# Mean embedding and projection: the running sum of rows in SBUF, low halves in one operation, seven product banks

## What is computed

```python
valid = sequence_ids < emb_table.shape[0]
safe_ids = jnp.where(valid, sequence_ids, 0)
seq_emb = emb_table[safe_ids] * valid[..., None]
denom = jnp.maximum(valid.sum(axis=1, keepdims=True), 1.0)
user_repr = seq_emb.sum(axis=1) / denom
logits = user_repr @ proj_w + proj_b
```

## Time and profile before

| | us |
|---|---|
| median of 3 runs | 642.86 (642.55 to 642.87) |
| the profiled execution | 643.35 |
| its span, first to last instruction | 641.6 |
| PE busy, 2602 matmul records | 609.1 (95%) |
| DVE busy | 407.9 (64%) |
| POOL busy | 233.6 (36%) |
| ACT busy | 137.6 (21%) |

### The profile page before, as it was taken

One profiled execution on the slowest core, in us unless ns is written; L12 is line 12 of the kernel. 1 busy time (PEld: TensorE's weight loads), 2 busy tenths in 40 slices (PEclk: granted clock), 3 DMA queues, 4 the chain that ended last, 5 costly groups with the idle time before them and its releaser, 6 DMA issues.

```text
span 641.6 us, 7583 instructions
## 1 busy us (share of the span) xinstructions
PE 609.1 (95%) x2602; PEld 476.1 (74%) x2602; DVE 407.9 (64%) x723; ACT 137.6 (21%) x153; POOL 233.6 (36%) x227
## 2 busy tenths in 40 slices
PE   1878799989999999999999999999999999999997
PEld 0326558777778787788788788888888888888886
DVE  7977958989878898697786454333333333344442
ACT  7605426132122131300200221110011111211210
POOL 5777777777764767566550000000000000000000
PEclk9999989999999999999999999999999999999999
DMA  9979999999998999798793398454555555566632
GB/s 311 388 259 331 380 390 293 373 329 318 315 296 298 305 291 313 236 323 249 236 341 121 97 288 260 127 173 161 177 176 177 176 177 176 171 185 201 223 127 103
DMA packets 77703, 158.31 MB, mean 247 GB/s; under 512 B 9287, under 2 KB 65042, under 8 KB 77658
## 3 DMA queue, kind: packets, MB, share of 16 engines
q1 hardware_dynamic: 60378, 110.30, 50.7%
q0 software_dynamic: 17280, 47.47, 23.2%
HBM read 115.70 MB, written 51.20 MB: 260 GB/s over the span
## 4 chain that ended last, share of the span: by engine, by line
PE 75%; DVE 13%; DMA 6%; issue 5%; ACT 1%; DVEq 1%; POOL 0%; POOLq 0%; ACTq 0%
PE acc L801 70%; DVE sums L539 5%; DMA rows<-in_L_rec_emb_table_dram,index 4%; PE turned L757 2%; DMA w_raw<-in_L_rec_proj_w_dram 2%; DVE w_lo L597 2%; DVE key L496 1%; DVE w_lo L595 1%; DVE top L492 1%; PE acc L806 1%; ACT w_hi L416 1%; DVE stage L609 1%; PE turned L749 1%; DVE mean L584 0%; PE turned L732 0%
## 5 line engine op out<-in xcount | busy, mean ns | idle before, releaser
L347 POOL DMA_INDIRECT rows<-in_L_rec_emb_table_dram,index x208 | 224.1, 1077 | 95.7 <-issue 58.1
L801 PE MATMUL acc<-w_hi,mean_hi 128*128 128x500 f32 x800 | 224.4, 402 | 0.8 <-ACT mean_hi L422 0.8
L609 DVE TENSOR_TENSOR stage<-acc,bias_sb 128x500 f32<-128x500 f32 x162 | 109.3, 676 | 179.4 <-PE acc L801 179.3
L801 PE MATMUL acc<-w_hi,mean_lo 128*128 128x500 f32 x800 | 213.8, 389 | 0.3 <-DVE mean_lo L589 0.3
L801 PE MATMUL acc<-w_lo,mean_hi 128*128 128x500 f32 x800 | 214.0, 389 | 0.0
L801 PEld LDWEIGHTS acc<-w_hi,mean_lo 128*128 128x128 f32 x800 | 150.1, 188 | 32.4 <-DVE mean_lo L589 1.6
L801 PEld LDWEIGHTS acc<-w_hi,mean_hi 128*128 128x128 f32 x800 | 150.2, 189 | 31.9 <-issue 4.3
L801 PEld LDWEIGHTS acc<-w_lo,mean_hi 128*128 128x128 f32 x800 | 150.2, 188 | 31.3
L539 DVE SCALAR_TENSOR_TENSOR sums<-rows,mask,sums 128x512 f32<-128x512 f32 x165 | 124.1, 752 | 8.8 <-DMA rows<-in_L_rec_emb_table_dram,index 0.6
L416 ACT ACTIVATE w_hi<-w_raw 128x2000 fp32r<-128x2000 f32 x39 | 72.9, 1875 | 236.3 <-PE acc L801 215.7
L595 DVE TENSOR_TENSOR w_lo<-w_raw,w_hi 128x1000 fp32r<-128x1000 f32 x39 | 46.5, 1193 | 13.4 <-ACT w_hi L416 13.3
(11 more groups left out here) (106 smaller groups left out, 180.9 us busy)
## 6 DMA issues: line engine op xcount, KB each, us to landing
out_dram<-stage SPq DMA_DIRECT2D x200, 250.0 KB, 3.8
w_raw<-in_L_rec_proj_w_dram SPq DMA_DIRECT2D x39, 1000.0 KB, 6.6
bias_sb<-in_L_rec_proj_b_dram SPq DMA_DIRECT2D x39, 250.0 KB, 4.9
raw_at_hi<-in_L_rec_proj_w_dram SPq DMA_DIRECT2D x4, 1000.0 KB, 11.1
rows<-in_L_rec_emb_table_dram,index POOLq DMA_INDIRECT x208, 5.8
raw_at_lo<-in_L_rec_proj_w_dram SPq DMA_DIRECT2D x3, 1000.0 KB, 13.7
stage<-in_L_rec_proj_w_dram SPq DMA_DIRECT2D x1, 1000.0 KB, 23.8
ids_sb<-in_r_sequence_ids_dram SPq DMA_DIRECT2D x1, 700.0 KB, 4.4
```

Source lines behind the costliest of these rows:

```text
L347: return pool.indirect_dma_start(out=dst, out_offset=None, in_=table, in_offset=bass.IndirectOffsetOnAxis(ap=column, axis=0), bounds_check ...
L609: dve.tensor_tensor(stage[:, g % STAGE, r - stores[g][0]], acc[:, r % BANKS, 0:BW], bias_sb[:, i % BIAS], ALU.add).then_inc(s_moved_by_dve, 1)
L801: last = nc.tensor.matmul(bank, first, second, start=part + k == 0, stop=part == 2 and k == K - 1 and not by_act[r])
```

## The change

- `sums` becomes an SBUF tensor of 128 x 512 floats. Every add of a column by DVE then reads two SBUF tensors (`rows` and `sums`) and writes SBUF, where it read `rows` from SBUF and `sums` from PSUM, and wrote PSUM.
- `rest_mean` is gone: ACT writes its share into `mean`, and DVE adds `sums` to it in place.
- `w_low` makes the low half of a block in one operation of 2000 elements.
- The PSUM bank that `sums` held goes to `acc`, which has seven banks. The small product `overs` at the start goes to one of them.

```diff
-    RAW, SPLIT, BIAS, ROWS, PLACED, BANKS = 2, 5, 4, 12, 2, 6
+    RAW, SPLIT, BIAS, ROWS, PLACED, BANKS = 2, 5, 4, 12, 2, 7
...
-        rest_mean = sb("rest_mean", [P, HID], F32)
         rows = sb("rows", [P, ROWS, HID], F32)
         mean = sb("mean", [P, HID], F32)
+        sums = sb("sums", [P, HID], F32)
...
-        sums = ctx.enter_context(nc.psum_tensor("sums", [P, HID], F32))
-        overs = sums[0:1]
 
         first_list = acc[:, BANKS - 1]
+        overs = acc[0:1, BANKS - 2]
...
-                nc.scalar.activation(rest_mean[:], turned[:], ACT.Copy,
+                nc.scalar.activation(mean[:], turned[:], ACT.Copy,
                                      scale=inv_count[:, t:t + 1]).then_inc(s_rest_mean, 1)
...
-                dve.tensor_scalar(rest_mean[:], sums[:], inv_count[:, 0:1], None, ALU.mult).then_inc(s_further_mean, 1)
+                dve.tensor_scalar(mean[:], sums[:], inv_count[:, 0:1], None, ALU.mult).then_inc(s_further_mean, 1)
...
-                dve.scalar_tensor_tensor(mean[:], sums[:], inv_count[:, t:t + 1], rest_mean[:], ALU.mult,
+                dve.scalar_tensor_tensor(mean[:], sums[:], inv_count[:, t:t + 1], mean[:], ALU.mult,
                                          ALU.add).then_inc(s_mean, 1)
...
                 dve.wait_ge(s_w_hi, q + 1)
-                half = K // 2
-                dve.tensor_tensor(w_lo[:, q % SPLIT, 0:half], raw(q)[:, 0:half],
-                                  w_hi[:, q % SPLIT, 0:half].bitcast(F32), ALU.subtract)
-                dve.tensor_tensor(w_lo[:, q % SPLIT, half:], raw(q)[:, half:],
-                                  w_hi[:, q % SPLIT, half:].bitcast(F32), ALU.subtract).then_inc(s_w_lo, 1)
+                dve.tensor_tensor(w_lo[:, q % SPLIT], raw(q), w_hi[:, q % SPLIT].bitcast(F32),
+                                  ALU.subtract).then_inc(s_w_lo, 1)
```

More of the change, by code:

```diff
@@ L577, in first_mean @@
                 dve.wait_ge(s_added, len(pe_columns[0]))
-                dve.scalar_tensor_tensor(mean[:], turned[:], inv_count[:, 0:1], rest_mean[:], ALU.mult,
+                dve.scalar_tensor_tensor(mean[:], turned[:], inv_count[:, 0:1], mean[:], ALU.mult,
                                          ALU.add).then_inc(s_mean, 1)
```

## The result

| | before | after |
|---|---|---|
| median, us | 642.7 (641.76 to 642.87, 4 runs) | 654.8 (653.89 to 655.15, 4 runs) |
| the profiled execution, us | 643.35 | 654.47 |
| its span, us | 641.6 | 652.7 |
| PE busy, us | 609.1 | 614.4 |
| DVE busy, us | 407.9 | 402.4 |

The account below looks back on a forecast made before the run. PE was taken to wait for POOL's gathered rows and DVE's means before transposes. Terms 7.6 + 1.3 + 0.7 - 0.5 = +9.1 us on the median 642.86 gave 652.0 us, range 645.0 to 656.5.

Parts of the forecast that it names:

- The hold: A DVE operation with two SBUF inputs holds a POOL gather starting inside it for its remaining time less 0.13 us.
- Tile 0 and tile 1: PE's columns of tile 1, tile 0's share included: later gathers make PE wait, +7.6 us (6.2 to 9.0).
- my rule that landings shrink when gathers lag behind the loads: Tile 1's last gather: landing of 4.1 us in place of 5.53.
- Tile 2: PE's two columns come 3.0 us later, the 1.73 us wait for the mean is swallowed: +1.3 us (0 to 2).
- Tile 3: DVE's columns: POOL 5.1 us behind against 3.7 us of slack, +0.7 us (0 to 1.4).
- Later tiles: Behind tile 3: gather holds are swallowed, DVE's gain at tiles 5 to 7 stays, -0.5 us.
- the gap between dependent columns: DVE's column adds: 0.07 us saved for each column directly following another, starts 0.785 us apart in place of 0.855.
- The banks: Seven product banks: PE has no wait for a bank, so an earlier free bank gives 0.
- Only the merged low halves hold: Rival: column adds hold no gather; tile 1 loses about 5.5 us, tiles 2 and 3 nothing; 647.4 us, chance 0.14.
- Loads set the landing: Rival: full DMA engines, not the issue, set when gathers land; holds cost nothing, 641.2 us, faster, chance 0.10.
- Gains and losses cancel: Rival: low-half holds half as large and landings shorter; within 1.3 us of 642.9, chance 0.06.
- The clock: Rival at tile 1's columns: granted clock falls again, up to +1.7 us, 653.7; chance 0.70 shared with the forecast.

Follow-up runs that it names:

- blocks 4 to 10 alone: Kernel before, with the low half in one operation for blocks 4 to 10 and in two elsewhere: 649.22 us, ratio 1.0092.
- six banks: Changed kernel with six product banks in place of seven, the eighth PSUM bank left unused: 653.79 us, ratio 1.0161 against the kernel before.
- the filling products: Changed kernel with six product banks and 14 unread bias products before PE's first column of tile 2: 652.55 us, ratio 1.0148 against the kernel before.
- the four pieces: Kernel before, with each block's low half in four operations of 500 elements in place of two of 1000: 643.34 us, ratio 0.9998.

## Why the prediction came out as it did

The sign, the mechanism and the place were right, and the median lies inside the range: 654.8, where 652.0 was forecast (+12.1 us for +9.1). By its own steps:

**The hold.** Right, but for a gather that starts first. Holds worked out by the rule "rest of the operation less 0.13" against recorded ones, as means over the gathers that start inside such an operation and that the rule would hold by more than 0.05 us:

| kernel | operation | gathers | rule, us | recorded, us |
|---|---|---|---|---|
| before | half of 1000, SBUF and SBUF | 21 | 0.763 | 0.714 |
| before | column, sum in PSUM | 61 | - | 0.000 |
| merged low half alone | low half of 2000 | 26 | 1.308 | 1.308 |
| after | low half of 2000 | 26 | 1.214 | 1.217 |
| after | column, sum in SBUF | 52 | 0.301 | 0.269 |
| sum in SBUF alone | column, sum in SBUF | 65 | 0.377 | 0.304 |

Where the recorded mean is below the rule, it is by gathers that weren't held at all: one of the 21, three of the 52 and eight of the 65. Each of them started within 0.10 us of the operation's recorded start. Without them the means agree within 0.004 us (0.746 and 0.750, 0.283 and 0.285, 0.347 and 0.347). In this case it is the DVE operation that lasts longer: those columns took up to 0.82 us in place of 0.75. Who starts first thus seems to decide it; the traces don't show why. The prediction's rule had no such case.

Over all 216 gathers the holds sum to 16.1 us before and 47.8 after. The Trainium skill's sentence that a VectorE instruction with two SBUF inputs contends with GpSimd's reads (page "SBUF — State Buffer", section "Who interferes with whom") agrees with these holds. Its inference that tensor_tensor leaves descriptor generation alone doesn't: the 26 gathers inside a low half of the changed kernel are such a case, at 1.22 us each.

**Tile 0 and tile 1: +7.6, measured +7.5.** Right in the sum, but by luck: the parts were off by up to 1.3 us and cancelled. Tile 0's last gather comes at 45.2, 1.8 us late (2.2 forecast). Tile 1's 27 gathers are busy for 37.3 us, not the 38 to 40 forecast: 5.8 more than before, where I took 6.8. The averages weren't off by much: seven merged low halves cost 5.5 us with blocks 4 to 10 alone, as forecast, and 6.4 with all merged; the columns alone cost just 17 x 0.15 = 2.6. But the two don't add up, for 5.5 + 2.6 = 8.1, and together they cost 5.8 here (6.4 with six banks, 5.4 with the filling products). A gather has one hold at a time, and in a row of columns gathers fall into step with DVE (1.20 to 1.22 us, a hold of 0.2, stands four times in tile 1). So the last gather is issued at 90.8, not 92.2. Its landing then took 5.4 us, not 4.1: my rule that landings shrink when gathers lag behind the loads didn't come true here, with the DMA share at 1.04 in the window from 81.3 to 91.5. In other kernels the same landing took 3.9 (six banks), 4.2 (merged low half alone) and 5.9 us (sum in SBUF alone), so its size is not something the lag alone sets. The chain of the changed kernel has a longer one yet, 0.85 us of it the hold:

```profile
82.11 7.21 DMA rows<-in_L_rec_emb_table_dram,index
```

**Tile 2: +1.3 (0 to 2), measured +4.6.** This is the step that failed. The gathers were forecast well (tile 2's last is 11.2 us later than before; I had 9.0 + 3.3 = 12.3). I let PE wait 3.0 us for its two columns and set the 1.73 us of the wait for the mean against that. I didn't ask what a gap of 3 us does to the clock there. I had looked for the clock at tile 1 only and priced it at 1.7 us. The run with 14 filling products shows 2.2 us of late rows, a little above the upper end given, and the distance from landing to transpose shows 2.4 us of the clock in the changed kernel (1.0 with six banks).

**Tile 3: +0.7, measured -0.8.** Its last column still has 2.55 us of slack, so nothing was added; the wait of 0.36 in the earlier trace rows is gone. Where the other 0.5 us come from is open.

**Later tiles: -0.5, measured -0.1.** A column's own time stayed as forecast (748 ns for 752), but the gap between dependent columns did not shrink: three columns in the changed kernel (timeline),

```profile
133.71 2.45 DVE L538 SCALAR_TENSOR_TENSOR sums<-rows,mask,sums 128x512 f32<-128x512 f32 x3
```

take 2.45 us where they took 2.46, a start every 0.852, not 0.785. The short wait behind L546 that I took this from belongs to another, smaller operation; what sets the gap is not shown. Only a tile's first column became quicker:

```profile
142.11 0.49 DVE L535 TENSOR_SCALAR sums<-rows,mask 128x512 f32<-128x512 f32 x1
```

It took about 0.75 us before; five of the seven take 0.48 to 0.49 now. The 5.5 us that DVE gained are thus made mostly of 47 low halves and seven first columns, and nearly all lie where PE doesn't wait for DVE.

**The banks.** 0 on what PE waits for; the 1.6 us between six and seven banks are not clear of noise and not settled.

**The rivals.** "Only the merged low halves hold" fell with the sum in SBUF alone (+2.9 us). "Loads set the landing" fell with the four pieces (an earlier issue gave an earlier transpose) and with the changed kernel (landing 5.4 in place of 5.5, 7.6 us later). "Gains and losses cancel" fell with the result itself, +12.1 us. "The clock" came true, but not where I looked for it: at tile 1 there are 10.2 us at 1.2 GHz in place of 3.4, and they cost nothing; at tile 2 there are 6.8, and they cost 2.4 us. So the forecast with this rival's 1.7 us, 653.7, comes near the 654.8 partly for a wrong reason.

## What to carry to other kernels

When gathers issued by POOL are what an engine waits for, the length of a single DVE operation with two SBUF inputs is a cost of its own: each gather that starts inside it (here, more than 0.10 us behind its start) is held nearly to its end, so keep such operations short or one of their inputs in PSUM there, and merge them only where no gather is late. When a change makes PE wait for a few microseconds where it didn't, look at every such place for the granted clock, not only at the one where it is low already, and ask whether PE has work there or only waits: a low clock during a wait that ends later anyway costs nothing. And a saving on an engine counts only at the waits that end with it: 5.5 us of DVE's time were saved here, and 12 us of the kernel's lost.

## What the runs showed of the hardware that was not expected

- The hold ends at the seam between two DVE operations that stand back to back, and 0.13 us ahead of the recorded end. A gather that starts within 0.10 us of the operation's start can escape it, and then DVE's operation is up to 0.07 us longer. Cutting the same 2000 elements into 1, 2 or 4 operations gives longest gathers of 3.04, 2.00 and 1.47 us.
- A sum in PSUM spares POOL entirely: of 61 gathers that start inside such a column, none is held, and DVE's copies of a unit, which read one tensor in PSUM and one in SBUF, hold none of 20 either. In SBUF the column is not quicker (748 against 752 ns) and holds gathers by 0.27 us on average.
- The clock can be held up by work of no use: 14 products of 3.1 us in a wait of 3.29 us kept the engine at 2.4 GHz. The work behind the wait took 1.0 us less for it; that the whole kernel gains (1.1 us between the medians) is not clear of noise.
